# An attention and FFN block on one core: the end of a prologue reordered around unread products, and the row-maximum passes one slot later

## What is computed

```python
q, k, v = heads(x @ Wq.T), heads(x @ Wk.T), heads(x @ Wv.T)    # 16 heads of 16
q, k = rope(q), rope(k)
scores = where(causal, q @ k.T / sqrt(16), -inf)
x = layernorm(x + merge(softmax(scores) @ v) @ Wo.T)
h = silu(x @ w_gate) * (x @ w_up)                              # 1024 wide
h = keep_the_2_largest_of_each_4(h)
x = layernorm(x + h @ w_down)
```

## Time and profile before

| | us |
|---|---|
| median of 3 runs (lowest to highest) | 724.06 (722.88 to 727.85) |
| profiled execution, its time | 722.13 |
| its span, first to last instruction | 720.4 |
| TensorE busy | 662.0 (92%) |
| VectorE busy | 561.4 (78%) |
| ScalarE busy | 406.1 (56%) |
| GpSimd busy | 316.9 (44%) |

### The profile page before, as it was taken

How to read it: one execution, slowest core, us unless ns; L and a number is a source line. 1 busy time by engine, 2 the same in 40 slices (tenths; PEclk the granted TensorE clock), 3 DMA queues, 4 the chain that set the end, 5 groups by cost and what they waited for, 6 DMA issues and landing times. The chain is left out here.

```text
span 720.4 us, 13794 instructions
## 1 busy us (share of the span) xinstructions
PE 662.0 (92%) x5264; PEld 489.3 (68%) x5264; DVE 561.4 (78%) x825; ACT 406.1 (56%) x578; POOL 316.9 (44%) x317
## 2 busy tenths in 40 slices
PE   7988788999999999998989988899999999999983
PEld 5665545656566665655546557698989898988873
DVE  5888656778786787877787386979898989798975
ACT  5650566676767777675666764545363536363522
POOL 4484876677767777632323133124132231404040
PEclk9996899999999999999999999999999999999998
DMA  4038536445555555558011102021120202010101
GB/s 127 30 101 182 143 111 195 129 139 171 136 173 157 151 161 150 149 155 278 26 60 34 59 1 89 30 88 59 31 65 23 87 0 87 0 59 0 59 1 58
DMA packets 48815, 67.61 MB, mean 94 GB/s; under 512 B 6456, under 2 KB 27448, under 8 KB 48760
## 3 DMA queue, kind: packets, MB, share of 16 engines
q1 hardware_dynamic: 47860, 65.23, 30.9%
q10 hardware_dynamic: 900, 1.64, 0.8%
HBM read 43.12 MB, written 23.07 MB: 92 GB/s over the span
## 5 line engine op out<-in xcount | busy, mean ns | idle before, releaser
L947 DVE TENSOR_REDUCE bmax<-mx_ps 128x8 f32<-128x1024 f32 (+1 forms) x148 | 180.8, 1222 | 76.0 <-PE mx_ps L1231 75.1
L784 ACT ACTIVATE prob<-ex_ps 128x1024 f32<-128x1024 f32 x160 | 163.7, 1023 | 85.4 <-PE ex_ps L1261 82.0
L614 POOL TENSOR_SCALAR_AFFINE_SELECT prob<-prob 128x512 f32<-128x512 f32 x128 | 84.7, 676 | 121.0 <-ACT prob L784 120.9
L1278 PE MATMUL pv_ps<-prob,v_sb 128*32 128x512 f32 (+3 forms) x1024 | 82.2, 439 | 1.2 <-POOL prob L614 1.2
L1216 PEld LDWEIGHTS mx_ps<-mask_b,half_id 64*128 64x128 bf16 x592 | 16.9, 94 | 77.6 <-DVE bmax L947 66.7
L1216 PE MATMUL mx_ps<-mask_b,half_id 64*128 64x128 bf16 x592 | 46.1, 235 | 21.3 <-DVE bmax L947 18.7
L1521 POOL TENSOR_TENSOR hm_l<-v_sb,hm_h 128x2048 fp32r<-128x2048 f32 x4 | 18.5, 4618 | 89.2 <-ACT hm_h L1582 89.2
L1521 POOL TENSOR_TENSOR k_st<-v_sb,q_st 128x2048 fp32r<-128x2048 f32 x3 | 13.9, 4623 | 75.5 <-ACT q_st L1582 75.5
L1278 PEld LDWEIGHTS pv_ps<-prob,v_sb 128*32 128x32 f32 x1024 | 25.4, 109 | 27.4 <-issue 23.3
L1568 ACT ACTIVATE g_sb<-ex_ps 128x512 f32<-128x512 f32 x28 | 16.5, 591 | 44.6 <-PE ex_ps L1784 44.6
L1830 PE MATMUL mi_ps<-wd_h,q_st 128*128 128x256 f32 x128 | 37.3, 291 | 3.4 <-DVE k_st L1700 3.4
(11 more groups left out here) (261 smaller groups left out, 1980.8 us busy)
## 6 DMA issues: line engine op xcount, KB each, us to landing
y_sb<-x SPq DMA_DIRECT2D x12, 512.0 KB, 4.0
xT_sb<-xT SPq DMA_DIRECT2D x8, 512.0 KB, 3.9
q_st<-q_parts SPq DMA_DIRECT2D x32, 128.0 KB, 2.7
k_st<-k_parts SPq DMA_DIRECT2D x32, 128.0 KB, 2.8
x<-y_sb SPq DMA_DIRECT2D x8, 512.0 KB, 3.2
xh<-x SPq DMA_DIRECT2D x8, 512.0 KB, 3.9
q_parts<-qk_rot SPq DMA_DIRECT2D x14, 256.0 KB, 3.2
k_parts<-qk_rot SPq DMA_DIRECT2D x14, 256.0 KB, 2.8
```

Source lines behind the costliest of these rows:

```text
L614: nc.gpsimd.affine_select(out=block, in_=block, compare_op=ALU.is_ge, fill=0.0, base=0, pattern=[[0, n], [1, P]], channel_multiplier=-1).t ...
L784: nc.scalar.activation(out, ex_ps[:], ACT.Exp).then_inc(ex_act, 1)
L947: nc.vector.tensor_reduce(out=out, in_=src, axis=AX.X, op=ALU.max).then_inc(mx_read, 1)
L1278: last = nc.tensor.matmul(pv_ps[32 * g:32 * g + 32, P * kt:], v_sb[b % 2][:, kt, G4 * j + g, :], probs(g), start=kt == 0, stop=kt == 2, sk ...
```

## The change

What belongs to the fills moves a slot later: `FILL_AT` from -25 to -24, and with it the transposes of the maxima ("nm" from -5 to -4), `negate_max` (-6 to -5) and `PLACE_AT`. Batch 1 has four fills in the prologue instead of five; the fifth stands in slot 0. A new prologue entry ("I", n, 0) issues n unread products into the bank of the next product. `keep_busy` takes its operands as arguments for that. Three of twelve rotation steps of batch 2 move from GpSimd's prologue into slots 2, 3 and 4 (`ROPE_2_AT`), and two of its four splits move a slot back.

```diff
-FILL_AT = -25
+FILL_AT = -24
...
-    ... ("nm", 0, -5),
+    ... ("nm", 0, -4),
...
+ROPE_2_AT = {9: 2, 10: 3, 11: 4}
...
-HIGH_2_AT, LOW_2_AT = [-40, -39, -37, -36], [-39, -38, -36, -35]
+HIGH_2_AT, LOW_2_AT = [-40, -39, -36, -35], [-39, -38, -35, -34]
...
-FIRST_FILLS = 5
+FIRST_FILLS = 4
 PROLOGUE = [
...
-    ("F", 0, 10), ("R", 0, 12), ("F", 0, 11), ("R", 0, 13), ("H", 1, 3), ("F", 0, 12), ("R", 0, 14),
-    ("F", 0, 13), ("R", 0, 15), *[("F", 0, f) for f in range(14, FILLS)], ("QK", 2, 0), ("nm", 0, 0),
-    ("F", 1, 0), ("QK", 2, 1), ("F", 1, 1), ("F", 1, 2), ("QK", 2, 2), ("F", 1, 3), ("F", 1, 4), ("QK", 2, 3),
+    ("F", 0, 10), ("R", 0, 12), ("F", 0, 11), ("R", 0, 13), ("H", 1, 3), ("F", 0, 12), ("R", 0, 14), ("I", 3, 0),
+    ("F", 0, 13), ("R", 0, 15), ("I", 2, 0), ("F", 0, 14), ("I", 2, 0), ("F", 0, 15), ("QK", 2, 0), ("F", 0, 16),
+    ("F", 0, 17), ("QK", 2, 1), ("F", 0, 18), ("F", 0, 19), ("I", 4, 0), ("nm", 0, 0), ("F", 1, 0), ("F", 1, 1),
+    ("QK", 2, 2), ("F", 1, 2), ("QK", 2, 3), ("F", 1, 3),
 ]
...
-PLACE_AT = [-4, -3]
+PLACE_AT = [-3, -2]
...
             for n in range(3 * NT):
-                rope_transposed(pool, nc.gpsimd, 2, n)
+                if n not in ROPE_2_AT:
+                    rope_transposed(pool, nc.gpsimd, 2, n)
...
+                for n, at in ROPE_2_AT.items():
+                    if g == at:
+                        rope_transposed(pool, nc.gpsimd, 2, n)
                 if 0 <= g < SLOTS * B:
                     mask(g // SLOTS, g % SLOTS)
...
-                if (b := batch_at(g, -6)) is not None and b > 0:
+                if (b := batch_at(g, -5)) is not None and b > 0:
                     negate_max(b)
...
-                    pe.wait_ge(mx_read, FILLS + FIRST_FILLS - 1)
+                    pe.wait_ge(mx_read, FILLS + FIRST_FILLS)
...
-            def keep_busy(g):
-                op, b, i = next(x for later in range(g + 1, G_TO) for x in misc_at(later))
+            def keep_busy(op, b, i, n):
                 out = start_bank(op, b, i)
-                for _ in range(IDLE):
+                for _ in range(n):
...
+                if op == "I":
+                    keep_busy(*next(x for x in PROLOGUE[n:] if x[0] not in "FHI"), b)
+                    continue
```

More of the change, by code:

```diff
@@ L49 @@
     ("Wo", 1, 40), ("V", 0, -18), ("V", 1, -18), ("O", 0, 23), ("V", 2, -16), ("V", 3, -16), ("O", 1, 25), ("O", 2, 25),
-    ("O", 3, 27), ("QK", 0, -51), ("QK", 1, -50), ("aT", 0, 32), ("aT", 1, 32), ("QK", 2, -46), ("nm", 0, -5),
+    ("O", 3, 27), ("QK", 0, -51), ("QK", 1, -50), ("aT", 0, 32), ("aT", 1, 32), ("QK", 2, -46), ("nm", 0, -4),
     ("QK", 3, -43), ("Wo", 0, 39),
@@ L131, in bank_uses @@
 def bank_uses():
-    order = [x for x in PROLOGUE if x[0] not in "FH"] + [x for g in range(G_FROM, G_TO) for x in misc_at(g)]
+    order = [x for x in PROLOGUE if x[0] not in "FHI"] + [x for g in range(G_FROM, G_TO) for x in misc_at(g)]
     return {x: (n % 3, n // 3 + 1) for n, x in enumerate(order)}
@@ L1356, in _ @@
             stay_ready(WARM_UP)
-            for op, b, i in PROLOGUE:
+            for n, (op, b, i) in enumerate(PROLOGUE):
                 if (op, i) == ("R", 0):
                     stay_ready(WARM_UP)
+                if op == "I":
+                    keep_busy(*next(x for x in PROLOGUE[n:] if x[0] not in "FHI"), b)
+                    continue
                 if op == "R":
@@ L1388, in _ @@
                 if last_at(g, IDLE_AT):
-                    keep_busy(g)
+                    keep_busy(*next(x for later in range(g + 1, G_TO) for x in misc_at(later)), IDLE)
 NK = I // P
```

## The result

| | before | after |
|---|---|---|
| median of the runs, us | 726.70 (20 runs, 722.46 to 731.22) | 733.52 (20 runs, 725.27 to 736.09) |
| profiled execution, us | 722.13 (span 720.4) | 734.86 (span 733.1) |
| mean granted clock, profiled | 0.979 | 0.965 |

The ratio after to before is 1.0073, with a 95% interval of 1.0046 to 1.0100; it is not the ratio of the two medians, which differ by 6.8 us (0.9%). So the change makes the kernel slower, by 5 to 7 us; 723 was predicted, a gain, and its widest range ended at 727. The times of the changed kernel fall into two groups, and the granted clock sorts them: six executions took 725.3 to 727.5 us at a mean clock of 0.977 to 0.979, thirteen took 732.5 to 736.1 at 0.965 to 0.967, and one lies between.

A forecast was written before the change was run, and what follows sets the result against it. Mostly the slot loop sets the time (fill, VectorE reduction, next fill; fuller slots by PE work), with two half-clock dips early. 722.13 - 2.2 - 1.2 + 2.6 = 721.3, on the median 723.2, said 723; own range 721 to 725, widest 718.5 to 727.

The forecast's parts named there:

- part 3: Slots of batches 1 to 7: fills and transposes of the maxima a slot later cost 2.6 us in all.
- Part 1: End of the prologue: clock stays full, maxima's transposes at about 63.6, slot 0's scores at about 71.2; gain 2.2 us.
- rival (b): Prologue: clock still falls near 51 or at 61 to 64 us, projections double; +3.0, 727 us; chance 0.2.
- Part 2: Slots 0 to 10: the 1.21 us wait for GpSimd goes, the second clock dip stays; gain 1.2 us.
- Part 4: Way from maxima to first scores: DMAs issued a slot later still land in time, margin 1.4 us, cost 0.
- Rival (c): Maxima's DMAs arrive late in every batch, landing over 3.4 us: up to +4, 727 us; chance 0.07.
- (d): Slot 16: transposes hide in PE gaps, part 3's loss goes, 2.6 below the forecast, 720.5 us; chance 0.08.

The follow-up runs named there:

- fills_only: The kernel before with fills, transposes of the maxima and PLACE_AT a slot later, batch 1's fifth fill in slot 0, prologue otherwise as before: 733.59 us, 1.0095.
- prologue_only: The changed kernel's prologue and rotation, but fills, transposes and DMAs in the slots of the kernel before: 726.84 us against 726.02, ratio 1.0000.
- before_again: The kernel before, unchanged, run once more for a second trace: 726.46 us, ratio 1.0000.
- best_early: prologue_only with pairs of unread products in first slots, eight products instead of four ahead of the transposes, last projection behind all fills: 723.81 us, 0.9953 of before.
- after_idle: The changed kernel with a pair of unread products added in slot 115 and slot 136's pair moved to 135: 728.05 us, 1.0005 of before.
- after_idle2: The changed kernel with pairs of unread products added in slots 115 and 135, five products instead of two in slot 134: 725.69 us, 0.9997 of before.
- prologue_warm: prologue_only with two unread products in each of slots 0, 1, 5, 7, 19 and 20: 724.90 us, 0.9985 of before.

## Why the prediction was wrong, point by point

Two terms failed, by 4.3 and 3.4 us: part 3's cost of the move (2.6 forecast, 6.9 in fills_only by its ratio) and the gain of parts 1 and 2 (3.4 forecast, nothing in prologue_only by its ratio, give or take 1.7).

**Part 3, the larger of the two.** The slots were costed by PE's work and VectorE's floor, and what the emptied slots do to the clock was put at nothing, without a word on it. The costed part nearly held: 3.2 us from slot 10 to 140 at a full clock, for 2.6. Slot 35 lasts 1.90 us and slot 36 2.82, and a batch in the steady part costs 0.3 (slots 40 to 60, 44.53 against 44.23) for 0.37 forecast; batch 6's 0.55 measured 0.54. By an estimate from these numbers (6.9 less 3.2) some 3.7 us are the clock's. What was missing:
- Slots 115 to 117 last 6.29 to 6.34 us in the traces of all five kernels in which slot 115 was emptied and left so, each with a fall there, and 4.16 to 4.18, with none, in all seven in which it was not. That is 2.1 us, of which the fall is 1.6: the difference to the 4.71 and 4.73 of the two kernels that have a pair of unread products there.
- Batch 7's slots 134 to 140: 0.2 forecast, 1.2 at a full clock, the 1.0 between them being in the main slot 134's 2.9 us for the 1.9 forecast; and 2.7 to 3.7 with a clock fall, which came in all four kernels with the fill in slot 135 and no pairs added (15.3 to 16.3 us). Of the eight without that fill five had none (12.61 to 12.64) and three did (14.1 to 15.6): the change makes it likelier, it doesn't bring it by itself.
- Falls elsewhere, slots 128 to 134 above all. I can't say that they are the change's alone: before_again's fall at slots 20 to 22 and prologue_only's from 366.5 to 370 and 376.5 to 383.5 stand in kernels whose slots there are as before.

**Part 1, 2.2 us forecast, -1.3 in this pair of traces.** The clock does hold near 51 us, as forecast: the idle pieces there are 0.77 and 0.17 us and not one of 1.90. The changed prologue at 49 to 52 us, and where its clock then falls:

```profile
49.79 0.97 PE L1336 MATMUL mi_ps<-wqkv_h 128*128 128x512 f32 x3 [0.77 <-DVE w_gate_parts L922]
50.93 0.34 PE L1222 MATMUL ex_ps<-mask_b,half_id 64*128 64x256 bf16 x4 [0.17 <-DVE bmax L953]
...
57.44 0.63 PE L1117 MATMUL mi_ps<-xl,wqkv_h 128*128 128x512 f32 x1
...
65.49 0.60 PE L1178 MATMUL mi_ps<-ident,nmax 128*16 128x128 f32 x4 [1.34 <-DVE nmax L959]
...
68.42 0.63 PE L1117 MATMUL mi_ps<-xh,wqkv_h 128*128 128x512 f32 x1
```

At a full clock the projection's products (L1117) take 0.39 to 0.40 us. It fell six microseconds later (56.9), on the first of the projections that had been put between the fills, and VectorE waited for the fill behind it:

```profile
59.61 1.23 DVE L953 TENSOR_REDUCE bmax<-mx_ps 128x8 f32<-128x1024 f32 x1 [1.75 <-PE mx_ps L1237]
...
64.99 0.35 DVE L959 TENSOR_REDUCE nmax<-bmax 128x64 f32<-128x192 f32 x1
```

The maxima's reduction starts at 64.99 where 63.2 was forecast and 62.95 had been. This is rival (b) in all but the place. Even with no fall ahead of 66 us, as in prologue_only, it starts at 63.92 and the transposes at 64.42, against 63.6 forecast and 64.19 before. So in that trace nothing is gained at this point: VectorE waits 0.61 and 0.28 us for the fills behind the two projections, about the 0.8 that the forecast had allowed, and its whole chain runs 0.3 us later than in the kernel before already at 51 us. Of the 3.5 us between slot 0's forecast start (71.2) and the measured one (74.74), 1.9 had been lost by the transposes (65.49 for 63.6) and 1.6 behind them. Then the wait of 1.34 us ahead of the transposes, which I had covered with four products in the sum but not for the clock, has the next fall behind it (67 to 70.4) on projection three.

All fourteen traces tell more than the pair. The six with the idle piece of 1.90 us ahead of fill 13 have a fall that begins between 50.8 and 53.1 us. None of the eight with the unread products has one there; six of them have it between 55.0 and 57.0, two only from 66.1 and 71.9. So the products moved the fall by some 5 us, and mostly did not remove it. And slot 10 begins at 98.06 to 99.29 in three traces with the prologue and first slots of before, and at 96.63 to 98.41 in four with those of the change: some 1.1 us gained on average, of the 3.4 forecast.

The way from the maxima to the first scores is a floor here too, and the forecast left it out. The maxima's DMAs land 5.1 to 7.4 us after the second is issued in the prologue; in best_early, after_idle and after_idle2 slot 0's scores start 0.09 us behind that landing. With the transposes at 63.6 and the issue 2.0 us behind them, as in the changed kernel (65.49 and 67.45), an estimate gives 70.7 to 73.0 for slot 0, so 71.2 was near the best case.

**Part 2, 1.2 us forecast, 1.0 measured**: slots 0 to 10 take 23.67 us against 24.64. The wait of 1.21 us for GpSimd is gone, and the second fall stayed, both as forecast. But the start was late, so slot 10 begins at 98.41 and not at 94.6; that is case (b)'s 98.5, though by another fall than the one that case named.

**Part 4 held for batches 1 to 6, not for batch 7.** At slots 20 to 120 the scores wait for no DMA in any trace, and slot 20 shows only the floor's 1.09 us of idleness; the landing behind the second issue takes 2.3 to 2.6 us there in the changed kernel, for the 2.0 forecast. Slot 140 is different:

```profile
390.70 0.52 ACTq L760 DMA_DIRECT2D q_st<-x1h_odd  x1
...
395.00 0.49 PE L1267 MATMUL ex_ps<-q_st,k_st 50*128 50x512 f32 x2 [0.26 <-issue]
```

The last update of `nm_dma` is at 394.91, 4.2 us after the issue, more than the 3.4 us of room that the forecast had. Five of the seven traces with the transposes a slot later have such a wait at slot 140, of 0.22 to 0.33 us, and none of the other seven. It is part of batch 7's 1.2 us. Rival (c), a late landing in every batch and up to 4 us, is out all the same. So is (d): slot 36 costs what was forecast.

**The sum.** Rival (b) came true for the prologue of the profiled execution and gave 727. The changed kernel's better executions, 725.3 to 727.5 us, are about that; whether by that way can't be said, as none of them was profiled. The larger group lies some 7 us further up, at the lower mean clock. Falls in the slots behind the prologue, which no case contained, are what its profiled member shows there. The Trainium skill's page "TensorE: Matmul & The Clock Gate", section "What's actually happening", was quoted for dips that need not sit at the same place in each execution. The traces bear that out, by the fall at 121.5 us in one execution of the kernel before and not in the other. I applied it to the prologue alone, where the profile had shown falls, and to no slot that the change made leaner.

**What stays open.** Which of the falls in slots 128 to 134 and behind slot 157 belong to the change; a profile shows one execution, and the falls of the others are known only by their mean clock. And why the fall at 56 us comes in most executions with the changed prologue: prologue_only and prologue_warm, whose order is the same up to there, went through without one.

## What to carry to other kernels

When work is moved out of a slot, ask what the engine's clock does with the emptiness before asking what the target slot pays: look for the next long piece of TensorE work behind the emptied one, and price it at half clock (here 1.50 to 2.79 us). Two unread products in the idle piece bought it back at slot 115 (6.29 to 4.71 us); so when a move leaves a slot lean, pad it in the same step, and look again, for in the first slots the pairs only moved the fall, and a pair in slot 135 came too late for a fall that the wait in slot 134 leaves behind. And read a floor per slot from the engine that sets it, at that slot: VectorE's 1.97 us of other work between two reductions made 2.9 out of 1.9.

## What the runs showed that I had not expected

A fall needs no long pause. It came behind idle pieces of 0.75 and 1.09 us (slots 114 and 115) and of 1.35 us (slot 134), between short bursts of matmuls, and the clock stayed at half for 3.4 to 7 us. The place varies between executions of one kernel, and with it the time: at a mean clock of 0.979 the changed kernel takes 725.3 us and at 0.965 it takes 736.1, so a comparison of two single traces charged the change with 12.7 us where the medians differ by 6.8.
